# Attention over all contexts: where three transposes of a unit stand, where a row sum stands, and 62 nops in VectorE's program

## The chip, the cores and the metric

The kernel runs on one core of a Trainium2 chip, in one launch. The metric is the device time of that core in microseconds (us). The core has TensorE (matmuls and transposes), VectorE, ScalarE, GpSimd and SyncE (which starts most DMAs). Each engine runs its own program in order, and they wait for each other by semaphores. Every engine's program comes into the engine by DMA while it runs.

## The reference, cut to what matters

The kernel computes a chain of eight residual blocks over x of 16 x 256 x 256 (4096 tokens of width 256), with a context of 16 x 120 tokens of width 192. The change is in the fifth block, an attention in which every token looks at all 1920 context tokens of the batch, in eight heads of width 128:

```python
qh = _split_heads(jnp.einsum('bnq,qi->bni', x, Wq))
kh = _split_heads(jnp.einsum('bmc,ci->bmi', context, Wk))
vh = _split_heads(jnp.einsum('bmc,ci->bmi', context, Wv))
sim = jnp.einsum('hid,hjd->hij', qh, kh) * SCALE
mean = jnp.mean(sim, axis=-1, keepdims=True)
sim = (sim - mean) * ATTN_MATRIX_SCALE + mean
attn = jax.nn.softmax(sim, axis=-1)
out = jnp.einsum('hij,hjd->hid', attn, vh)
return jnp.einsum('bni,iq->bnq', out, Wout) + bout
```

Here `x` is the layer-normed input, and the result is added to it. The blocks before it are an attention with an int8 feed-forward, a second attention and a block of experts; behind it come a ternary feed-forward, a selective block (cross attention that keeps the best 32 scores of a row, with a convolution in frequency space) and an attention over chosen tokens.

## The kernel before

`STAGES` lists the stages; each writes one program for each engine. VectorE's programs of all stages lie one behind the other, so what is added in an early stage moves the code of all later ones. Loops over batches or heads are `Fori` loops of the hardware, whose body is written once and which end in a branch back; the rest is written out. Such loops are at L481 (first stage, 13 passes), L919 (second attention, 14), L1330 and its like (experts, 16), L1642 (heads 1 to 6 of the global attention) and L2371 (selective stage, 5 passes, two batches each).

The changed stage is `global_attention_stage` (L1439). A unit is 512 queries (four token tiles of 128, `QT` = 4) against one head, `n = h * QUADS + t`, with eight units (`QUADS`) to a head and eight heads, so 64 units. The 1920 keys are four chunks of 480 (`chunks`) for the scores and 15 tiles of 128 (`KT`) for the attention. Two units are in work at once, interleaved by token tile j = 0 to 3:

- of unit n+1, `scores(n + 1, ., j)`: four PSUM banks (0 to 3), one for each chunk, three f32r matmuls each (L1849 to L1851). VectorE takes the maximum of each bank (`maximum`, L1695), then of the four, and scales it to the bias of the exponential (L1697, L1698). ScalarE waits for the bias and runs four exponentials (`exponential`, L1801), each with a read of its accumulator that yields the row sum. An exponential frees its bank for the scores of tile j+1, by the semaphore `exped`.
- of unit n, for the key tiles k of this j (`shares[j]`, four of them, three for j = 3): TensorE transposes the probabilities of tile k+2 (`turn`, four 128x128 transposes into bank 4 or 5, L1891) and multiplies tile k with the values, three matmuls into bank 6. ScalarE copies each transposed bank to its f32r high part (`high_probs`, L1780), VectorE takes the low part by a subtraction (`low_probs`, L1689); tile k's matmuls, and the transposes of k+2 into the same bank, wait for its low part (`low_ready`).

At j = 0 TensorE runs all four score banks of unit n+1, then waits until the last exponential of unit n is there (`exped`) and transposes tiles 0 and 1 of unit n; then comes `output(n - 1, 0)`, and then tile 0, which waits for its low part. VectorE at j = 0 does the maximum over all four banks, then `sums` (adds the parts of the row sums and takes the reciprocal, L1719 and L1720), then low 0, low 1, `output(n - 1, 0)` (two operations that add to x_res, L1728), low 2 and so on. At j = 3 TensorE runs the four score banks, transposes tile 14, and multiplies tiles 12, 13 and 14. VectorE at j = 3 does the maximum, then low 14. ScalarE at j = 3 does high 14, then the four exponentials, then the copy of the attention result (L1832).

At j = 2 the queries of unit n+2 are made (`queries`, `high_queries`, `low_queries`). In a head's last unit (`turns_head`, t = 7) the keys of the next head stand where the scores of tile 0 would, and the scores of tile 0 come behind key tile 1; the values of the next head are made in it too. `before` and `after` are false for the first and the last unit of all.

The lines of VectorE's order at L1742 to L1757, and of TensorE's at L1911 to L1922, are those that the change touches:

Of the kernel before, what the change touches and what calls it, by code (L numbers as in the profile page):

```python
# [385 lines left out]
def attention_and_int8_stage(nc, w, ctx):  # L386
# [80 lines left out]

    scores = w.psum[:, 0:per, 0:parts * NCTX].rearrange("p r (k j) -> p r k j", j=NCTX)
    v_bank, k_bank, prob_t_banks, attn_bank, out_bank = 2, 3, (4, 5), 4, 5
    xn_t_bank, q_bank = 6, 7  # L470
    int8_bank = (v_bank, k_bank)
    AHEAD, BEHIND = 5, 6
# [14 lines left out]
    with nc.allow_non_contiguous_dma(reason="rows of a weight for each part"), nc.Block() as block:  # L487
# [57 lines left out]
        @block.vector  # L545
        def _(dve):
            chain = Chain(dve, w.chains["dve"])

            def prepare_weight8():
                dve.wait_ge(weight8_loaded.sem, 16)  # L550
# [888 lines left out]
def global_attention_stage(nc, w, ctx):  # L1439
# [8 lines left out]
    chunks = B // 4  # L1448
    KEYS = B * NCTX
    KT = KEYS // P  # L1450
    QT = 4
# [194 lines left out]
    with nc.Block() as block:  # L1646
# [36 lines left out]
        def _(dve):  # L1683
# [4 lines left out]
                dve.wait_ge(high_is_ready.sem, high_is_ready.count(n))  # L1688
                dve.tensor_tensor(dst, psum, high.bitcast(F32), ALU.subtract).then_inc(ready.sem, 1)  # L1689

            def maximum(n, j):

                for c in range(chunks):
                    dve.wait_ge(scores_psum.sem, scores_psum.count((n * QT + j) * chunks + c))
                    ins = dve.tensor_reduce(top[:, c:c + 1], w.psum[:, c, 0:chunk], AX.X, ALU.max)  # L1695
                chain.link(ins)
                chain.link(dve.tensor_reduce(bias[:, j % 2:j % 2 + 1], top[:, :], AX.X, ALU.max))  # L1697
                dve.tensor_scalar(bias[:, j % 2:j % 2 + 1], bias[:, j % 2:j % 2 + 1], -scale, None,  # L1698
                                  ALU.mult).then_inc(bias_ready.sem, 1)
# [32 lines left out]
            def head(h, first, last):  # L1732
                chain.restart_always()
                for t in range(QUADS):
                    n = h * QUADS + t
                    before, after = not (first and t == 0), not (last and t == LAST)
                    turns_head = t == LAST and after
                    for j in range(QT):
                        if turns_head and j == 0:
                            for c in range(chunks):  # L1740
                                low_keys(h + 1, c)
                        elif after:  # L1742
                            maximum(n + 1, j)
                        if j == 0:
                            sums(n, t)
                        if j == 1 and before:
                            output(n - 1, (t - 1) % QUADS, 1)
                        if j == 2 and not (last and t >= LAST - 1):
                            low_queries(n + 2, t % 2)
                        for k in turned_in[j]:  # L1750
                            if k == 2 and before:
                                if first and t == 1:
                                    dve.wait_ge(bias_added.sem, bias_added.count(0))
                                output(n - 1, (t - 1) % QUADS, 0)
                            if turns_head and k == 4:
                                maximum(n + 1, 0)
                            low_probs(n, k)  # L1757
                            if t == 0 and k == 7:
                                low_values(h, 3, 7)
                            if turns_head and k in (7, 11, 14):  # L1760
                                low_values(h + 1, (7, 11, 14).index(k), 7)
# [82 lines left out]
        def _(pe):  # L1844
# [28 lines left out]
                                     start=(k == 0), stop=(k == DK - 1))  # L1873
                last.then_inc(q_psum.sem, 1)

            def scores(n, par, j, new_keys=None, fresh=False):
                tokens = slice(j * P, (j + 1) * P)
                if j == 0:
                    pe.wait_ge(q_ready.sem, q_ready.count(n))
                for c in range(chunks):  # L1880
                    if new_keys is not None and j == 0:
                        pe.wait_ge(k_ready.sem, k_ready.count(new_keys * chunks + c))
                    else:
                        pe.wait_ge(exped.sem, exped.count((n * QT + j - 1) * chunks + c))
# [21 lines left out]
            def head(h, first, last):  # L1906
                for t in range(QUADS):
                    n = h * QUADS + t
                    before, after = not (first and t == 0), not (last and t == LAST)
                    turns_head = t == LAST and after  # L1910
                    for j in range(QT):  # L1911
                        if turns_head and j == 0:
                            for c in range(chunks):
                                keys(h + 1, c, (n * QT + QT - 1) * chunks)
                        elif after:
                            scores(n + 1, (t + 1) % 2, j)
                        if j == 0:
                            pe.wait_ge(exped.sem, exped.count((n * QT + QT) * chunks - 1))
                            if first and t == 0:
                                pe.wait_ge(v_ready.sem, v_ready.count(2))  # L1920
                            turn(n, t % 2, 0)
                            turn(n, t % 2, 1)  # L1922
                        if j < 2 and before:
                            if j == 0 and t == 0:
                                pe.wait_ge(v_ready.sem, v_ready.count(h * QT + 2))
# [11 lines left out]
                        for k in shares[j]:  # L1937
                            if t == 0 and k % 4 == 0:
                                pe.wait_ge(v_ready.sem, v_ready.count(h * QT + k // 4))
                            pe.wait_ge(low_ready.sem, low_ready.count(n * KT + k))  # L1940
                            if k + 2 < KT:
                                turn(n, t % 2, k + 2)
                            last_mm = three_passes(w.psum[:, 6, :], (v_high[:, k, :], v_low[:, k, :]),
                                                   (prob_t_high[:, k % RING, :], prob_t_low[:, k % RING, :]),
# [1468 lines left out]
```

## Time and profile before

| | us |
|---|---|
| median of 3 runs | 4376.85 (4372.74 to 4380.01) |
| the profiled execution | 4377.85 |
| its span | 4376.0 |
| TensorE busy | 4032.5 (92%) |
| VectorE busy | 3192.7 (73%) |
| ScalarE busy | 2292.7 (52%) |
| GpSimd busy | 557.0 (13%) |

The span is the time from the first to the last instruction of the profiled execution. Busy time is what an engine spends in its instructions; TensorE's matmuls overlap, and the end of one is modelled. The global attention lies between some 1514 and 3364 us of the span, the selective stage's loop between 3629 and 4004 us. In rows of the trace an L-number is a line of the kernel before; "PE" is TensorE, "DVE" VectorE, "ACT" ScalarE; a trailing q is the engine's sequencer, which runs branches and register operations.

### The profile page before, as it was taken

To read this page: it belongs to the slowest core of one execution; us is meant where nothing else is said; L and a number is where in the kernel's file an instruction comes from. 1 tells how busy PE (TensorE), PEld (TensorE's weight loads), DVE (VectorE), ACT (ScalarE), POOL (GpSimd) and SP (SyncE) were. 2 spreads that over 40 slices of the span, in tenths; PEclk is the share of its full clock that TensorE was granted. 3 is DMA by queue.
4 is the path that set the end of the run, shared out by engine and by line. 5 is a ranking of instruction groups with operands and counts; after the bars stand their busy time and mean duration, and the time that the engine had idled before them with its cause. 6 is when DMAs were issued, how large, how long until landed. Compare 5 with 4: busy or idle time off the path is not lost. (4 is left out here: it accounts for less than half of the span.)

```text
span 4376.0 us, 69715 instructions
## 1 busy us (share of the span) xinstructions
PE 4032.5 (92%) x23076; PEld 3186.9 (73%) x23076; DVE 3192.7 (73%) x7663; ACT 2292.7 (52%) x5416; POOL 557.0 (13%) x1081
## 2 busy tenths in 40 slices
PE   6997997999889999999999999999999678889788
PEld 5886775777668777777777777787787456666565
DVE  6996666676657777777777777777777588889457
ACT  3554664555555565555655656555565134444344
POOL 1331001101130000000000000000033422232211
PEclk9998998999989999999999999999999589999899
DMA  3001000000000000000000000000000200000001
GB/s 98 0 0 39 0 0 1 0 0 0 18 4 1 3 3 2 5 1 6 1 2 5 2 5 1 2 5 2 2 1 12 66 1 1 1 1 1 15 27 39
DMA packets 34282, 40.67 MB, mean 9 GB/s; under 512 B 6272, under 2 KB 30474, under 8 KB 33934
## 3 DMA queue, kind: packets, MB, share of 16 engines
q1 hardware_dynamic: 33200, 36.90, 2.9%
q8 instruction: 137, 2.24, 0.2%
q14 instruction: 145, 1.19, 0.1%
q10 hardware_dynamic: 800, 0.33, 0.0%
HBM read 32.77 MB, written 4.19 MB: 8 GB/s over the span
## 5 line engine op out<-in xcount | busy, mean ns | idle before, releaser
L1780 ACT ACTIVATE global_prob_t_high<-psum 128x512 fp32r<-128x512 f32 x960 | 569.8, 601 | 586.9 <-PE psum L1891 586.9
L1689 DVE TENSOR_TENSOR global_prob_t_low<-psum,global_prob_t_high 128x512 fp32r<-128x512 f32 x960 | 656.6, 689 | 252.4 <-ACT global_prob_t_high L1780 238.1
L1695 DVE TENSOR_REDUCE global_top<-psum 128x1 f32<-128x480 f32 x1024 | 666.2, 657 | 115.4 <-PE psum L1851 109.9
L1849 PE MATMUL psum<-global_prob_t_high,global_v_low 128*128 128x512 f32 x960 | 455.7, 475 | 0.8
L1849 PE MATMUL psum<-global_k_high,global_q_low 128*128 128x480 f32 x1024 | 391.2, 382 | 15.0 <-ACT spare L1801 13.0
L1851 PE MATMUL psum<-global_k_high,global_q_high 128*128 128x480 f32 x1024 | 392.1, 383 | 0.0
L1850 PE MATMUL psum<-global_k_low,global_q_high 128*128 128x480 f32 x1024 | 389.1, 380 | 0.0
L1850 PE MATMUL psum<-global_prob_t_low,global_v_high 128*128 128x512 f32 x960 | 379.6, 395 | 0.0
L1851 PE MATMUL psum<-global_prob_t_high,global_v_high 128*128 128x512 f32 x960 | 379.4, 395 | 0.0
L1801 ACT ACTIVATE spare<-psum,global_bias 128x480 f32<-128x480 f32 x512 | 337.1, 663 | 17.5 <-DVE global_bias L1698 16.0
L1801 ACT ACTIVATE global_prob<-psum,global_bias 128x480 f32<-128x480 f32 x512 | 337.2, 662 | 1.3
L1367 ACT ACTIVATE moe_gated<-psum,moe_weight 128x256 f32<-128x256 f32 x512 | 214.8, 471 | 228.6 <-PE psum L1421 213.3
L1891 PEld LDWEIGHTS psum<-ident,global_prob 128*128 128x128 f32 x1920 | 233.6, 141 | 99.3 <-DVE global_prob_t_low L1689 34.6
L1891 PEld LDWEIGHTS psum<-ident,spare 128*128 128x128 f32 x1920 | 233.6, 141 | 96.4 <-DVE global_prob_t_low L1689 33.5
L1891 PE MATMUL psum<-ident,global_prob 128*128 128x128 f32 x1920 | 284.1, 273 | 18.8 <-DVE global_prob_t_low L1689 17.8
L1891 PE MATMUL psum<-ident,spare 128*128 128x128 f32 x1920 | 283.9, 273 | 18.0 <-DVE global_prob_t_low L1689 18.0
L374 POOL COPY powers<-ones 128x128 f32<-128x128 f32 x1 | 0.4, 414 | 1942.6 <-PE psum L1872 1942.6
L1849 PEld LDWEIGHTS psum<-global_k_high,global_q_low 128*128 128x128 f32 x1024 | 194.0, 189 | 56.1 <-ACT spare L1801 14.2
L1850 PEld LDWEIGHTS psum<-global_k_low,global_q_high 128*128 128x128 f32 x1024 | 193.4, 189 | 34.2 <-issue 0.2
L1851 PEld LDWEIGHTS psum<-global_k_high,global_q_high 128*128 128x128 f32 x1024 | 193.7, 189 | 29.5
L1851 PEld LDWEIGHTS psum<-global_prob_t_high,global_v_high 128*128 128x128 f32 x960 | 180.6, 188 | 42.3
L1419 PE MATMUL psum<-moe_we_high,moe_xn_low 128*128 128x512 f32 x512 | 204.3, 399 | 0.0
(486 smaller groups left out, 8335.1 us busy)
## 6 DMA issues: line engine op xcount, KB each, us to landing
x_res<-in_x SPq DMA_DIRECT2D x8, 512.0 KB, 10.1
moe_we<-in_expert_t SPq DMA_DIRECT2D x8, 512.0 KB, 7.5
out<-x_res SPq DMA_DIRECT2D x16, 256.0 KB, 2.1
cho_wqkv<-in_L_ffn_Wqkv SPq DMA_DIRECT2D x2, 1536.0 KB
self_ctx_t<-in_ctx_t SPq DMA_DIRECT2D x2, 1440.0 KB, 13.4
sel_w<-in_L_xattn_W SPq DMA_DIRECT2D x2, 1024.0 KB, 10.4
global_ctx_t<-in_ctx_t SPq DMA_DIRECT2D x1, 1440.0 KB
sel_ctx_t<-in_ctx_t SPq DMA_DIRECT2D x1, 1440.0 KB
```

The costliest lines, as they stand in the source:

```text
L374: pool.tensor_copy(re[:, :, 0], w.ones[:, :])
L1367: last = act.activation(gated[:, local % RING, h, :], w.lane(s)[:, 1 + p % 3, h * D:(h + 1) * D], ACT.Relu, scale=weight[:, s, x:x + 1])
L1419: pe.matmul(bank, xn_low[:, s, k, :], we_high[pair], start=False, stop=False)
L1689: dve.tensor_tensor(dst, psum, high.bitcast(F32), ALU.subtract).then_inc(ready.sem, 1)
L1695: ins = dve.tensor_reduce(top[:, c:c + 1], w.psum[:, c, 0:chunk], AX.X, ALU.max)
L1780: act.activation(dst, psum, ACT.Copy).then_inc(ready.sem, 1)
L1801: act.activation(prob[par][:, j, c * chunk:(c + 1) * chunk], w.psum[:, c, 0:chunk], ACT.Exp, bias=bias[:, j % 2:j % 2 + 1], scale=scale, a ...
L1849: pe.matmul(to, lhs_low, rhs_high, start=start, stop=False)
L1850: pe.matmul(to, lhs_high, rhs_low, start=False, stop=False)
L1851: return pe.matmul(to, lhs_high, rhs_high, start=False, stop=stop)
L1891: last = pe.transpose(w.psum[:, 4 + k % 2, j * P:(j + 1) * P], prob[par][:, j, k * P:(k + 1) * P], w.ident[:, :])
```

## The change

In TensorE's program the transposes of tiles 0 and 1 go from behind the four score banks of token tile 0 to between the third and the fourth, with their wait for the last exponential; the transposes of tile 14 go from behind the four score banks of token tile 3 to between the third and the fourth, with a wait for the low part of tile 12. In VectorE's program low 0 and low 14 go between the maximum of the third and of the fourth bank. Where no scores stand at that place (the head's last unit at j = 0, the last unit of all) the order stays. `sums` goes from j = 0 to j = 2, behind the maximum. ScalarE's program stays. In the first stage, which is `attention_and_int8_stage`, 62 `engine_nop` are put ahead of all else in VectorE's program.

```diff
+    FETCH_FILL = 62
...
             chain = Chain(dve, w.chains["dve"])
+            for _ in range(FETCH_FILL):
+                dve.engine_nop()
...
-            def maximum(n, j):
+            def maximum(n, j, within=None):
 
                 for c in range(chunks):
+                    if within is not None and c == chunks - 1:
+                        low_probs(n - 1, within)
                     dve.wait_ge(scores_psum.sem, scores_psum.count((n * QT + j) * chunks + c))
...
                         elif after:
-                            maximum(n + 1, j)
-                        if j == 0:
-                            sums(n, t)
+                            maximum(n + 1, j, within={0: 0, QT - 1: KT - 1}.get(j))
                         if j == 1 and before:
                             output(n - 1, (t - 1) % QUADS, 1)
+                        if j == 2:
+                            sums(n, t)
...
-                            low_probs(n, k)
+                            if not (after and (k == KT - 1 or (k == 0 and not turns_head))):
+                                low_probs(n, k)
...
-            def scores(n, par, j, new_keys=None, fresh=False):
+            def scores(n, par, j, new_keys=None, within=None):
...
                 for c in range(chunks):
+                    if within is not None and c == chunks - 1:
+                        within()
...
+                    def first_turns():
+                        pe.wait_ge(exped.sem, exped.count((n * QT + QT) * chunks - 1))
+                        if first and t == 0:
+                            pe.wait_ge(v_ready.sem, v_ready.count(2))
+                        turn(n, t % 2, 0)
+                        turn(n, t % 2, 1)
+
+                    def last_turn():
+                        pe.wait_ge(low_ready.sem, low_ready.count(n * KT + KT - 3))
+                        turn(n, t % 2, KT - 1)
...
+                            first_turns()
                         elif after:
-                            scores(n + 1, (t + 1) % 2, j)
-                        if j == 0:
-                            pe.wait_ge(exped.sem, exped.count((n * QT + QT) * chunks - 1))
-                            if first and t == 0:
-                                pe.wait_ge(v_ready.sem, v_ready.count(2))
-                            turn(n, t % 2, 0)
-                            turn(n, t % 2, 1)
+                            scores(n + 1, (t + 1) % 2, j, within={0: first_turns, QT - 1: last_turn}.get(j))
+                        elif j == 0:
+                            first_turns()
...
-                            if k + 2 < KT:
+                            if k + 2 < KT and not (after and k + 2 == KT - 1):
                                 turn(n, t % 2, k + 2)
```

## Rows read from the trace of the kernel before

**Rows 1.** TensorE's timeline, 2149 to 2163 us: start, duration, engine, line, operation.

```profile
2149.13 0.38 PE L1849 MATMUL psum<-global_k_high,global_q_low 128*128 128x480 f32 x1
...
2151.73 0.60 PE L1891 MATMUL psum<-ident,spare 128*128 128x128 f32 x4
...
2153.33 0.40 PE L1851 MATMUL psum<-global_prob_t_high,global_v_high 128*128 128x512 f32 x1
2153.74 0.50 PE L1849 MATMUL psum<-global_prob_t_high,global_v_low 128*128 128x512 f32 x1
...
2154.56 0.37 PE L1849 MATMUL psum<-global_k_high,global_q_low 128*128 128x480 f32 x1
...
2159.62 0.66 PE L1891 MATMUL psum<-ident,global_prob 128*128 128x128 f32 x4 [0.57 <-DVE global_prob_t_low L1689]
2160.04 0.48 PE L1849 MATMUL psum<-global_prob_t_high,global_v_low 128*128 128x512 f32 x1
...
2162.31 0.48 PE L1849 MATMUL psum<-global_prob_t_high,global_v_low 128*128 128x512 f32 x1
```

**Rows 2.** VectorE's timeline from 2145 us; in brackets idle time and who ended it.

```profile
2145.41 0.69 DVE L1689 TENSOR_TENSOR global_q_low<-psum,global_q_high 128x512 fp32r<-128x512 f32 x1 [1.31 <-ACT global_q_high L1780]
...
2149.98 2.61 DVE L1695 TENSOR_REDUCE global_top<-psum 128x1 f32<-128x480 f32 x4
...
2152.82 0.15 DVE L1698 TENSOR_SCALAR global_bias<-global_bias 128x1 f32<-128x1 f32 x1
...
2158.36 0.17 DVE L1719 TENSOR_REDUCE global_inverse<-global_part_sum 128x4 f32<-128x16 f32 x1
...
2158.88 1.29 DVE L1689 TENSOR_TENSOR global_prob_t_low<-psum,global_prob_t_high 128x512 fp32r<-128x512 f32 x2
2160.08 0.86 DVE L1728 SCALAR_TENSOR_TENSOR x_res<-psum,global_inverse,x_res 128x256 f32<-128x256 f32 x2
2160.95 0.69 DVE L1689 TENSOR_TENSOR global_prob_t_low<-psum,global_prob_t_high 128x512 fp32r<-128x512 f32 x1
```

**Rows 3.** ScalarE's timeline over the same seam.

```profile
2152.37 0.60 ACT L1780 ACTIVATE global_prob_t_high<-psum 128x512 fp32r<-128x512 f32 x1 [2.48 <-PE psum L1891]
2153.00 0.66 ACT L1801 ACTIVATE global_prob<-psum,global_bias 128x480 f32<-128x480 f32 x1
2153.56 0.19 ACT L1801 ACTIVATION_READ_ACCUMULATOR global_prob<-psum,global_bias 128x1 f32 x1
...
2154.93 0.67 ACT L1801 ACTIVATE global_prob<-psum,global_bias 128x480 f32<-128x480 f32 x1
...
2160.32 0.60 ACT L1780 ACTIVATE global_prob_t_high<-psum 128x512 fp32r<-128x512 f32 x1 [0.80 <-PE psum L1891]
```

**Rows 4.** A head's first matmul; and TensorE's branches of L1642 (min/median/max ns).

```profile
2057.07 0.48 PE L1849 MATMUL psum<-global_k_high,global_q_low 128*128 128x480 f32 x1 [1.36 <-ACT spare L1801]
...
L1642 PEldq COMPARE_BRANCH  x3: 3446/3557/3897, 1782.2 to 2324.4; - x3
```

**Rows 5.** A pass of the selective loop: busy us of PE, PEld, DVE, ACT, POOL.

```profile
3778.00:3853.00 75.00, 66.69 (x295) 50.20 (x294) 65.63 (x272) 34.30 (x70) 21.95 (x42) 0.98 0.00 1
```

**Rows 6.** Selective loop: VectorE's branches and moves (ns, first and last start), timelines.

```profile
L2371 DVEq COMPARE_BRANCH  x5: 55/63/74, 3701.0 to 4004.0; - x5
L2371 DVEq MOVE  x4: 36/36/36, 3704.0 to 3931.5; - x4
...
3780.85 0.69 DVE L2536 TENSOR_TENSOR spare<-psum,spare 128x512 f32<-128x512 f32 x1 [3.37 <-remote]
...
3781.74 5.38 PE L2769 MATMUL psum<-powers,sel_forward 128*128 128x256 f32 x16 [3.72 <-DVEq L2537]
```

**Rows 7.** Instruction DMAs of that pass; all DMAs, 100 to 315 us.

```profile
q14 instruction: 5, 0.04, 0.2%
...
DMA packets 0, 0.00 MB, mean 0 GB/s; under 512 B 0, under 2 KB 0, under 8 KB 0
```

**Rows 8.** VectorE's timeline early in the kernel.

```profile
20.21 0.29 DVE L265 TENSOR_TENSOR ssm_states<-ssm_states 128x128 f32<-128x128 f32 x1 [12.18 <-DMA ssm_states<-in_c_im_t]
```

## The prediction

> **What bounds the kernel now.** I read first the page's busy times, by which TensorE comes first and VectorE next. Then the three engines' timelines over one seam between two units of the global attention, 2149 to 2163 us [rows 1 to 3]. A unit is 512 queries against one head. Ordinary units (of which the trace holds 48) repeat every 32.00 us, at the full clock of 2.4 GHz. Within one, TensorE runs matmul after matmul but for two places: it waits 0.57 us before the attention of key tile 0 (2159.62, for `low_probs` of tile 0), and it starts tile 14 at 2153.74 where 2153.33 plus a step of 0.23 would allow 2153.56, so 0.18 late. So TensorE bounds most of a unit, and a chain VectorE, ScalarE, VectorE bounds the seam. Last, the selective stage, because the added nops shift VectorE's whole program: there VectorE is busy 65.6 of 75 us [rows 5], the densest engine with its links, and TensorE waits 3.72 us for it in each pass [rows 6].
>
> I count times from P, the first score matmul of token tile 3 (2149.13), in us.
>
> **Part 1, the last transpose earlier.** Now: scores to P+2.60, transposes of tile 14, then attention of 12, 13, 14 [rows 1]; VectorE takes the maximum of the four banks in one go (P+0.85 to P+3.46), the bias is written by the operation at P+3.69, and low 14 runs behind that [rows 2]. After: the transposes go in at the start of the fourth bank, P+1.95 (nine score matmuls of 0.217). ScalarE's high 14 starts 0.64 behind them (2152.37 against 2151.73) and takes 0.60 [rows 3]: P+2.59 to 3.19; low 14 0.03 later for 0.69: P+3.22 to 3.91. VectorE had the third bank done at P+2.81 and idles 0.41. TensorE no longer waits at tile 14, and gains its 0.18. But what is queued behind low 14 is the maximum of the fourth bank, P+3.92 to 4.57 (2.61/4 each); the bias operation starts 0.23 behind it, P+4.80 (it did at P+3.69), so **the bias is 1.11 us later**. Who waits for it: ScalarE's four exponentials, which free the score banks. The first starts 0.18 behind the bias operation (2153.00 against 2152.82), at P+4.98; the others follow in 0.643 steps (2153.00 to 2154.93 is three). Its signal is given when the accumulator read behind it ends, 0.75 after its start, and TensorE starts 0.05 later (as 2159.57 to 2159.62): **P+5.78**. TensorE now starts the next unit at P+5.43, with its bank free since P+4.67; it could after start at P+5.25, but must wait to P+5.78. So the slack of 0.76 is used up and 0.35 is lost here.
>
> **Part 2, the first transposes earlier.** They need the fourth exponential, P+4.98+1.93+0.80 = P+7.71; the banks are paced by the exponentials till then. High 0 starts 0.70 behind, P+8.41 (as 2160.32 behind 2159.62, also from a standing start), low 0 at P+9.04 to 9.73 (now at 2158.88, P+9.75: 0.7 earlier, so TensorE's 0.57 us wait at tile 0 goes). What is late next: the fourth maximum now lies behind low 0, P+9.74 to 10.39; bias operation P+10.62; low 1 0.17 behind it, about as the exponential, P+10.79; `output` 0.61 after low 1 starts (2158.88 and 0.60 per tile to 2160.08), P+11.40; low 2 0.87 later (2160.08 to 2160.95), P+12.27 to 12.96. Now low 2 ends at P+12.51 (2160.95+0.69). TensorE needs it for tile 2, whose attention starts at 2162.31, P+13.18, its transposes 0.35 before. After: transposes at 12.96+0.05 = P+13.01 from a standing start, attention 0.41 later (as 2159.62 to 2160.04 in the same unit): P+13.43. So the attention of tile 2 comes **0.24 us later per unit** than now; behind it TensorE is the bound as before. For 48 units (t = 1 to 6 of eight heads): +11.5 us. Bounds: 0.1 to 0.4 per unit, 5 to 19 us, since eleven hand-overs of a few hundredths each are in the chain.
>
> **Part 3, sums later.** Two small operations and their link, 0.49 us between the bias and low 0 (2158.36 to 2158.88 less the 0.03 hand-over [rows 2]), go behind the third tile's maximum, where VectorE waits 1.31 us for ScalarE's high queries (2145.41): cost nothing; without that cover 0.5 per unit. The gain is already in part 2's chain (without it low 1 would be 0.49 later). In the seven units t = 7, where keys and not scores stand first, it takes some 0.4 off TensorE's wait and meets the 0.35 to 0.45 lost at the unit's start: 0.
>
> **Head boundaries.** At the six back branches of the loop over heads TensorE stands for 1.36 us [rows 4], though the exponential that the row names was long done: TensorE's sequencer is 3.4 to 3.9 us in the branch itself. TensorE reaches the branch when low 14 is there, which comes up to 0.65 earlier; VectorE restarts when it does now. Between 0.2 and 0.47 gain for each, say -2.2 with the seventh; the last unit pays 0.7 for its later exponentials. The attention together: 11.5 + 0 - 2.2 + 0.7 = **+10.0**.
>
> **Part 4, 62 nops.** They stand ahead of VectorE's first work; a little later it idles 12.18 us in a row for a DMA [rows 8], which covers 62 nops of up to 0.19 us each: nothing. What they do is to move all later VectorE code by 62 places. VectorE's instructions come by DMA in blocks of 8 KB, one for every 128 records of its trace. Its loop in the selective stage has 328 records per pass (272 busy ones [rows 5]) and by the fetch times lies over four blocks: 48 records in the first, 36 in the last. At each of its four back branches the branch takes 63 ns, but the next instruction comes 2.98, 2.93, 2.96 and 2.81 us later (3701.0 to 3704.0 [rows 6]), and 5 blocks are fetched in each pass [rows 7]. VectorE's next work waits 3.37 us, and TensorE 3.72 us for VectorE [rows 6], so this is on the path. Moved by 62 (any shift from 48 to 92 would do) the loop lies in three blocks. Do three stay resident, with the fourth fetched ahead? Loops that cross one block edge stay: between 100 and 315 us, twelve passes of a loop whose ScalarE part crosses an edge, nothing is fetched at all [rows 7], so at least three blocks are held. A fourth no row shows; the refetch of all four blocks in every pass fits three or four held. I take the gain, since the loop would then ask for one block less than the smallest number excluded: (11.68 - 4 x 0.14) = **-11.1 us**; bounds 0 and -12.
>
> By the Trainium skill, "Runtime: NRT & Kernel Launch", section "Instruction fetch mechanics", an engine holds 32 KiB in two lines of 256 instructions, and a taken branch outside them stalls for a fetch. The trace differs in the line (8 KB). Read as 32 KiB in 8 KB blocks it is four, and the stall goes; read as only two pages it stays, which is the first rival.
>
> **Sum.** 4377.85 (the profiled execution, span 4376.0; the runs' median is 4376.85) + 10.0 - 11.1 = 4376.8, by the median about **4376**. Within 0.2% (8.8 us) of now, which is about what a measurement can tell from no change.
>
> **Rivals.**
> First, slower: the selective loop's stall stays, as three blocks and the one fetched ahead don't fit. For it: no row shows a loop over three blocks. It decides from the first back branch: if that costs 2.9 us, 4376.85 + 10 = 4387.
> Second, faster: the late bias hides. For it: TensorE's bank is free 0.76 us early now, and the two waits that the change aims at go, 0.57 + 0.18 = 0.75 in some 55 units, 41 us; with the nops' 11 it would be 4325. Against it: bias 1.11 later is more than 0.76. With hand-overs shorter than I take, anything up to 4365.
> Third: the chain costs 0.4 to 0.5 a unit, since TensorE restarts at four banks: 4388 to 4395.
> Fourth: the shift splits loops that lay in one block (attention and experts stages, 27 back branches) and these stall, 27 x 2.9 = 78 us: 4455. Against it the ScalarE loop above.
>
> **Chances.** Forecast 0.45 (4368 to 4386), first rival 0.22, second with all between 0.22, third 0.08, fourth 0.03. Of the forecast a tenth or more lies below 4368. Faster 0.30, same 0.44, slower 0.26. The range leaves out the far ends of the second and the fourth: 4355 to 4391.
>
> **What would show it.** Right: ordinary units 32.24 apart; at the seam TensorE waiting for ScalarE's exponential before the first bank and for low 1 and low 2; no wait at tile 14; the bias of tile 3 at P+4.8; in the selective loop VectorE's move within 0.2 us of the branch. Wrong: units under 32.0 (part 1 hides), or moves 3 us behind the branch (part 4 fails).

## The result, and the profile after

Five runs of each kernel in turn: before 4376.85 us (4372.74 to 4380.01), changed 4357.05 us (4353.84 to 4358.71), ratio 0.9953 with a 95% interval of 0.9939 to 0.9968. The change makes the kernel 0.47% faster. The forecast was 4376, no difference that can be measured; 4357 lies near the lower end of its range, 4355 to 4391, and the case that it took for the likeliest (4368 to 4386) did not come about.

| us | before | changed | difference | forecast |
|---|---|---|---|---|
| the profiled execution | 4377.85 | 4357.05 | -20.8 | -1.1 |
| its span | 4376.0 | 4355.2 | -20.8 | |
| first stage, until TensorE's program of it ends | 355.7 | 359.2 | +3.5 | 0 |
| global attention | 2169.4 | 2168.1 | -1.3 | +10.0 |
| ternary stage | 98.4 | 97.3 | -1.1 | 0 |
| selective stage | 653.6 | 632.3 | -21.3 | -11.1 |
| TensorE, VectorE, ScalarE busy | 4032.5, 3192.7, 2292.7 | 4034.9, 3172.7, 2291.0 | | |

The stages are cut where the drain starts that closes TensorE's program of each. The kernels of the experiments whose attention is that of before took 2169.4 to 2172.0 us for it, so the -1.3 of this row says little; the units below say more. The ternary stage varies as much (96.5 to 99.8 us over all kernels). So almost all of the gain is the selective stage's, where nothing was changed but the place of VectorE's code, and the attention, where all the reordering was done, is as long as before.

**The selective loop.** VectorE's branches and moves of the loop's line (L2390 now), which answer to [rows 6]: minimum, median and maximum in ns, then the first and the last start.

```profile
L2390 DVEq COMPARE_BRANCH  x5: 50/56/74, 3700.5 to 3983.6; - x5
L2390 DVEq MOVE  x4: 36/36/36, 3700.8 to 3913.2; - x4
```

The first branch starts at 3700.5 and the move behind it at 3700.8; before, the pair was 3701.0 and 3704.0. From first to fifth branch it is 283.1 us, before 303.0: a pass takes 70.8 us in place of 75.7 (76.6 the first, 75.5 the others). Busy time in a stretch of 75 us, a pass and a part of the next (columns: PE, PEld, DVE, ACT, POOL, then TensorE's granted clock, DMA share, GB/s), which answers to [rows 5]:

```profile
3773.00:3848.00 75.00, 69.31 (x316) 52.45 (x315) 69.22 (x283) 35.69 (x73) 26.35 (x53) 1.00 0.00 0
```

and all DMA of the same stretch, which answers to [rows 7]:

```profile
DMA packets 0, 0.00 MB, mean 0 GB/s; under 512 B 0, under 2 KB 0, under 8 KB 0
```

No instruction is fetched any more (5 a pass before), and the granted clock is 1.00 where it was 0.98. TensorE at the place where it waited 3.72 us for VectorE:

```profile
3772.77 3.69 PE L2788 MATMUL psum<-powers,sel_forward 128*128 128x256 f32 x16 [1.03 <-DVEq L2556]
```

Its wait is 2.69 shorter, as the gap behind the branch is. But the 16 matmuls behind it take 3.69 us and took 5.38: another 1.69, which the forecast knew nothing of. Before, the granted clock was the lower of the two levels, 1.2 GHz, for a good part of those matmuls:

```profile
3778.00:3781.70 3.70, 0.03 (x1) 0.00 (x0) 0.81 (x2) 0.38 (x1) 0.00 (x0) 1.00 0.01 4
3781.70:3783.70 2.00, 1.96 (x6) 1.66 (x7) 1.67 (x7) 0.00 (x0) 0.87 (x3) 0.66 0.00 0
3783.70:3785.70 2.00, 2.00 (x6) 1.53 (x6) 0.97 (x4) 1.09 (x2) 1.72 (x7) 0.50 0.00 0
3785.70:3787.70 2.00, 1.86 (x11) 1.41 (x9) 1.07 (x2) 0.10 (x1) 1.08 (x3) 0.98 0.00 0
```

These are stretches of the kernel before: 3.70 us with next to no matmul, then 0.66, then 0.50 (1.2 GHz), then 0.98, nearly the full clock again. Together they hold 3.4 us at 1.2 GHz, in which 1.7 us of work are lost, as much as the matmuls took more. Wait and matmuls are 4.4 of the 4.7 us that a pass gained; where the other 0.3 lies was not traced.

**The seam of two units.** TensorE of the changed kernel, P = 2152.14; it answers to [rows 1]:

```profile
2152.14 0.38 PE L1857 MATMUL psum<-global_k_high,global_q_low 128*128 128x480 f32 x1
...
2154.09 0.60 PE L1901 MATMUL psum<-ident,spare 128*128 128x128 f32 x4
...
2157.83 0.49 PE L1857 MATMUL psum<-global_k_high,global_q_low 128*128 128x480 f32 x1 [0.38 <-ACT global_prob L1809]
...
2159.90 1.04 PE L1901 MATMUL psum<-ident,global_prob 128*128 128x128 f32 x8
...
2162.29 0.60 PE L1901 MATMUL psum<-ident,global_prob 128*128 128x128 f32 x4
...
2164.87 0.66 PE L1901 MATMUL psum<-ident,global_prob 128*128 128x128 f32 x4
2165.28 0.48 PE L1857 MATMUL psum<-global_prob_t_high,global_v_low 128*128 128x512 f32 x1
```

and VectorE over the same stretch, which answers to [rows 2]:

```profile
2155.35 0.69 DVE L1694 TENSOR_TENSOR global_prob_t_low<-psum,global_prob_t_high 128x512 fp32r<-128x512 f32 x1 [0.41 <-ACT global_prob_t_high L1788]
2155.96 0.65 DVE L1702 TENSOR_REDUCE global_top<-psum 128x1 f32<-128x480 f32 x1
2156.64 0.16 DVE L1704 TENSOR_REDUCE global_bias<-global_top 128x1 f32<-128x4 f32 x1
2156.83 0.15 DVE L1705 TENSOR_SCALAR global_bias<-global_bias 128x1 f32<-128x1 f32 x1
...
2162.65 0.15 DVE L1705 TENSOR_SCALAR global_bias<-global_bias 128x1 f32<-128x1 f32 x1
2162.75 0.69 DVE L1694 TENSOR_TENSOR global_prob_t_low<-psum,global_prob_t_high 128x512 fp32r<-128x512 f32 x1
2163.35 0.87 DVE L1735 SCALAR_TENSOR_TENSOR x_res<-psum,global_inverse,x_res 128x256 f32<-128x256 f32 x2
2164.14 0.68 DVE L1694 TENSOR_TENSOR global_prob_t_low<-psum,global_prob_t_high 128x512 fp32r<-128x512 f32 x1
```

This is the picture that the forecast drew, step for step: no wait at tile 14, a bias of token tile 3 that is late (P+4.69, before P+3.69), the next unit's scores waiting for ScalarE's exponential (P+5.69), and the attention of tile 2 waiting for low 2. Only it comes at P+13.14 and not at P+13.43, and it was P+13.18 before: the units are 31.96 apart, 0.04 less than before.

### The profile page after: what moved, and what is told of

Its sections match the earlier page's. It is cut to its first block and busy times, and to the rows that moved or that the text cites. A ratio compares the mean times of both kernels' runs of the same rounds, so it can differ in the third digit from the quotient of the medians.

```text
span 4355.2 us, 69783 instructions
## 1 busy us (share of the span) xinstructions
PE 4034.9 (93%) x23076; PEld 3171.0 (73%) x23076; DVE 3172.7 (73%) x7663; ACT 2291.0 (53%) x5416; POOL 563.7 (13%) x1081
## 3 DMA queue, kind: packets, MB, share of 16 engines
q14 instruction: 126, 1.03, 0.1%
## 5 line engine op out<-in xcount | busy, mean ns | idle before, releaser
L1857 PE MATMUL psum<-global_prob_t_high,global_v_low 128*128 128x512 f32 x960 | 445.0, 464 | 0.0
L1857 PE MATMUL psum<-global_k_high,global_q_low 128*128 128x480 f32 x1024 | 406.2, 397 | 32.8 <-ACT spare L1809 21.0
```

The lines of the kernel that those rows point to most:

```text
L1857: pe.matmul(to, lhs_low, rhs_high, start=start, stop=False)
```

## The experiments

Times are medians. The kernels with the 62 nops alone, with the new order alone and with both gains ran four to eleven times, all others once; with these the trace shows where the time went. The kernel before was run again beside each group: 4378.53, 4378.09 and 4380.36 us. "Units" are the ordinary ones (t = 1 to 6) of the looped heads.

**The nops alone.** The kernel before with

```diff
             chain = Chain(dve, w.chains["dve"])
+            for _ in range(62):
+                dve.engine_nop()
```

> The kernel before with the 62 nops and nothing else. Theory (VectorE's code layout makes the selective stage's gain, stall and what follows it): the four passes of the selective loop take 70.8 us as in the changed kernel (75.5 before), VectorE's move comes within 0.3 us of its branch, the stage loses 21.3 us; the first stage is 3.5 us longer, as in the changed kernel, because its VectorE loop now crosses a block edge; the attention's ordinary units stay at 32.00. Sum: 4376.85 - 21.3 - 1.1 + 3.5 = 4358, some 0.43% less than before, and within 3 us of the changed kernel. Rival (the extra 10 us of the selective stage come from somewhere else, such as the attention's new order or an execution's own variation): a gain of about 11 us, 4366. Second rival, on the first stage: its 3.5 us are noise of that execution, then 4354.

Measured: 4360.05 us, ratio to before 0.9956 (0.9943 to 0.997). Passes 70.8, gap 0.25, selective stage 633.5 us. The whole gain of the changed kernel within its uncertainty comes from 62 instructions that do nothing. The first stage ended at 360.4.

**The new order alone.** The changed kernel with

```diff
-    FETCH_FILL = 62
+    FETCH_FILL = 0
```

> The changed kernel with 0 nops: the attention's new order alone. Theory (a unit is 0.03 to 0.05 shorter, not the 0.24 longer that was forecast): units 31.96, the attention stage about 1.3 us shorter than before; selective passes back at 75.5 with a 2.9 us gap behind each branch; time 4376.85 - 1.3 = 4375.5, no difference that can be measured. Rival 1 (the forecast's price of the chain holds, and the execution seen was lucky): units 32.24, 4387. Rival 2 (the order is worth several us, hidden by something that the nops do): 4370 or less.

Measured: 4377.69 us, ratio 0.9998 (0.9988 to 1.0007), units 31.96, attention 2166.9 us, passes 75.5 with gaps of 2.8. The three moves together are worth nothing. Why nothing, when each of them moves something, is what the next three kernels ask.

**The sums alone.** The kernel before with

```diff
-                        if j == 0:
-                            sums(n, t)
                         if j == 1 and before:
                             output(n - 1, (t - 1) % QUADS, 1)
+                        if j == 2:
+                            sums(n, t)
```

> The kernel before with the row sums at token tile 2 and nothing else of the change. Theory (the two operations of the sums stand in the chain that TensorE waits for at key tile 0): low 0 starts 0.49 earlier, TensorE's wait of 0.57 before the attention of tile 0 shrinks to 0.08, and nothing is lost elsewhere, since the maximum and the bias keep their times: ordinary units 31.51, the attention stage 48 x 0.49 = 23 us shorter than before, time about 4354 without any nops. Rival (another chain is right behind, such as output and low 2 on VectorE): units 31.7 to 32.0, and the gain is under half of that.

Measured: 4352.53 us, units 31.57 in looped and written-out heads alike, attention 2142.6 us, 26.8 less than before. TensorE at the seam, P = 2108.87:

```profile
2117.78 1.03 PE L1902 MATMUL psum<-global_wo,global_attn_t 128*128 128x256 f32 x4
2118.92 0.66 PE L1891 MATMUL psum<-ident,spare 128*128 128x128 f32 x4
```

and VectorE:

```profile
2117.99 0.15 DVE L1698 TENSOR_SCALAR global_bias<-global_bias 128x1 f32<-128x1 f32 x1
2118.18 1.29 DVE L1689 TENSOR_TENSOR global_prob_t_low<-psum,global_prob_t_high 128x512 fp32r<-128x512 f32 x2
```

Low 0 starts 0.19 behind the bias operation; before it was 0.64, from this bias operation to the low 0 at 2158.88 [rows 2]:

```profile
2158.24 0.15 DVE L1698 TENSOR_SCALAR global_bias<-global_bias 128x1 f32<-128x1 f32 x1
```

TensorE starts the transposes of tile 2 at P+10.05, before at P+10.49 [rows 1]. All of it reaches the unit: 0.43.

**Sums and first transposes; sums and last transpose.** Both are the changed kernel without nops; the first puts the last transpose and low 14 back, the second the first transposes and low 0. The cores of the two edits, TensorE's alone (VectorE's low 14, or low 0, goes back with them):

```diff
-        scores(n + 1, (t + 1) % 2, j, within={0: first_turns, QT - 1: last_turn}.get(j))
+        scores(n + 1, (t + 1) % 2, j, within={0: first_turns}.get(j))
...
-        scores(n + 1, (t + 1) % 2, j, within={0: first_turns, QT - 1: last_turn}.get(j))
+        scores(n + 1, (t + 1) % 2, j, within={QT - 1: last_turn}.get(j))
+        if j == 0:
+            first_turns()
```

> The changed kernel without the nops and with the last transpose back behind the four banks: sums and the first two transposes alone. Theory (the late bias comes from low 14 ahead of the fourth maximum, so it is gone here, and what the first transposes still cost is low 2, which comes at most 0.2 after TensorE wants it): units 31.5 to 31.6, far below the 31.96 of all three moves. Rival (the first transposes are what costs): units 31.9 or more.

> The changed kernel without the nops and with the first transposes back behind the four banks: sums and the last transpose alone. Theory (the bias 1.0 later paces the next unit's banks by the exponentials, to a fourth bank 0.7 or more later than before; the sums' 0.49 make up for most of it): units 31.8 to 32.0, the late bias of token tile 3 at 4.7 us behind the tile's first score matmul. Rival (the late bias hides in the 0.76 us by which the bank is free early): units 31.4 or less, as TensorE's 0.18 wait at tile 14 goes too.

Measured: with the first transposes 4351.44 us, units 31.58, attention 2143.4; with the last transpose 4377.44 us, units 31.92, attention 2167.3. VectorE at the seam of the second, P = 2152.12:

```profile
2155.34 0.69 DVE L1694 TENSOR_TENSOR global_prob_t_low<-psum,global_prob_t_high 128x512 fp32r<-128x512 f32 x1 [0.41 <-ACT global_prob_t_high L1788]
...
2156.82 0.15 DVE L1705 TENSOR_SCALAR global_bias<-global_bias 128x1 f32<-128x1 f32 x1
```

and TensorE's first matmul of the next unit:

```profile
2157.82 0.48 PE L1857 MATMUL psum<-global_k_high,global_q_low 128*128 128x480 f32 x1 [0.39 <-ACT global_prob L1809]
```

The bias comes at P+4.70 as in the changed kernel, and TensorE waits for the exponential. In the first of the two kernels the wait at tile 0 is gone: the transposes of tile 2 start 0.86 behind the first output matmul, with the sums alone 1.14. But those of tiles 3 and 4 start 0.31 and 0.42 behind the attention matmul ahead of them, with the sums alone 0.23 and 0.24, so 0.26 of the 0.28 is lost again to low 1 and low 2, which come later: the first transposes are worth nothing. So the price of the change is almost all in one of its parts: sums -0.43 a unit, first transposes +0.01, last transpose +0.35 (31.92 against 31.57) or +0.38 (31.96 against 31.58).

| kernel | unit | attention stage |
|---|---|---|
| before | 32.00 | 2169.4 |
| sums | 31.57 | 2142.6 |
| sums, first transposes | 31.58 | 2143.4 |
| sums, last transpose | 31.92 | 2167.3 |
| sums, both (changed, no nops) | 31.96 | 2166.9 |

**How the place of the loop decides: 128, 100 and 40 nops.** Each is the kernel before with another number in `range(...)`.

> The kernel before with 128 nops: the selective loop lies over four blocks of 8 KB again, but with the other parity. Theory (blocks of 8 KB count, and four of them in a loop are too many): passes stay at 75.5, gap 2.9 us, about five instruction fetches a pass. Rival (16 KB lines of 256 instructions, two of which are held, as the Trainium skill, Runtime: NRT & Kernel Launch, section Instruction fetch mechanics, has it): before, the loop lay over three such lines (one block, two, one); moved by half a line it lies over two, and the stall goes: passes 70.8, gap under 0.3 us. First stage: no crossing, so as before (355.7).

> The kernel before with 100 nops. Theory (the loop lies in three blocks for a shift of 48 to 92 only; at 100 its last 8 records reach into a fourth): the stall is back, passes 75.5, gap 2.9 us, although there are more nops than in the changed kernel. Rival (any shift, or the nops as such, help): passes 70.8. Rival of 16 KB lines: by parity either; told together with the kernel of 128 nops. The first stage's VectorE loop crosses no edge at 100 and should end at 355.7 to 356 as before, not at 359.2.

> The kernel before with 40 nops. The forecast's condition was a shift of 48 to 92; 100 works too, so its upper end was wrong by at least 8 places. This asks for the lower end. Forecast's geometry (48 records of the loop in its first block): 8 of them remain in a block of their own, four blocks, passes 75.5, gap 2.9. Corrected geometry (block edges counted back from the fetches of the kernels with 62 and 100 nops, where the edge ahead of the loop stands 35 records before it at 62 nops, so 13 at 40): three blocks, passes 70.8, gap 0.25.

VectorE's branches and moves of the loop with 40 nops:

```profile
L2373 DVEq COMPARE_BRANCH  x5: 55/63/74, 3701.9 to 4003.6; - x5
L2373 DVEq MOVE  x4: 36/36/36, 3704.8 to 3931.4; - x4
```

with 100:

```profile
L2373 DVEq COMPARE_BRANCH  x5: 50/56/74, 3701.9 to 3985.0; - x5
L2373 DVEq MOVE  x4: 36/36/36, 3702.2 to 3914.5; - x4
```

and with 128:

```profile
L2373 DVEq COMPARE_BRANCH  x5: 55/63/74, 3702.7 to 4005.1; - x5
L2373 DVEq MOVE  x4: 36/36/36, 3705.5 to 3932.6; - x4
```

The page's row of fetched blocks in the whole program (packets, MB), with 40 nops (with 128 it is the same row, and 145 before):

```profile
q14 instruction: 146, 1.20, 0.1%
```

and with 100 (the same row with 62):

```profile
q14 instruction: 126, 1.03, 0.1%
```

At 40 and 128 the stall is there (4375.38 and 4379.16 us), at 62 and 100 it is gone (4358.72 us with 100). 128 nops, a whole block, restore the state before, so it is the place within a block of 8 KB that counts, and lines of 16 KB don't: 128 nops move the loop by half such a line, and in one of the two places two such lines would have held it. My expectation for 100 was wrong, and the forecast's own counts show why: with 328 records in the loop and 48 in its first block, 24 and not 36 are left for the fourth (48 + 128 + 128 + 24), so any shift from 48 to 104 would do and not only to 92. The trace with 100 nops agrees: the edge behind the loop shows some 5 records behind its last. The "corrected" count that I then made for 40, from the times of fetches, was wrong as well; these stood up to some 20 records off the edge. With the condition 48 to 104 all four come out: 40 no, 62 yes, 100 yes, 128 no.

**Where the other 2 us of a pass went: a delay without a fetch.** The kernel with 62 nops alone, and in the loop

```diff
             def iteration(M, T, F, now, done):
                 chain.restart_always()
+                if now and not isinstance(now[0], int) and now[1] == 0:
+                    for _ in range(4):
+                        link(dve.tensor_tensor(prod[0], by_cos[:, :, :], by_cos[:, :, :], ALU.mult))
```

> The kernel before with the 62 nops, and at the top of each pass of the selective loop four linked VectorE multiplications of 128x512 that nothing reads (0.69 us each with its link 0.7, so 2.8 us: as long as the stall that the nops took away, 2.98 less 0.25, but without any fetch). It asks where the rest of the 4.7 us per pass went, of which the gap behind the branch is only 2.7. Theory (TensorE's long idle: it waits 3.8 us, its granted clock falls to 1.2 GHz, and the 16 matmuls behind the wait take 5.4 instead of 3.7 us): passes 75.4, PEclk 0.50 in the two us behind the wait. Rival (the rest belongs to the fetches themselves, not to the idle): passes 73.6, the 16 matmuls 3.7 us.

> The same with two multiplications, 1.4 us: TensorE's wait becomes 2.4 us. Theory (the clock falls only behind a longer idle): passes 70.8 + 1.4 = 72.2, clock 1.00 behind the wait. Rival (any idle lengthened costs clock in proportion): passes 73.1. It brackets the idle at which the clock is lost between 2.4 and 3.7 us, or below 2.4.

The added work with four:

```profile
3787.28 2.87 DVE L2536 TENSOR_TENSOR powers<-sel_by_cos 128x512 f32<-128x512 f32 x4 [0.60 <-DVE sel_mean L2527]
```

TensorE's matmuls behind it, with four:

```profile
3791.16 5.27 PE L2774 MATMUL psum<-powers,sel_forward 128*128 128x256 f32 x16 [3.94 <-DVEq L2542]
```

and with two:

```profile
3785.34 6.50 PE L2774 MATMUL psum<-powers,sel_forward 128*128 128x256 f32 x16 [2.49 <-DVEq L2542]
```

Measured: 4386.47 us and passes of 75.1 to 75.4 with four, 4380.61 us and 75.07 with two. The first is as the theory has it: a delay of 2.87 us that fetches nothing costs 4.5 us, and the matmuls take 5.27. So the rest of the loss is the clock's, behind the longer wait, and needs no fetch. The second missed both expectations. With half the delay TensorE's wait is 2.49 us and the pass is just as long, because the 16 matmuls now take 6.50 us. The granted clock of the kernel with two:

```profile
3784.00:3786.00 2.00, 0.66 (x2) 0.60 (x3) 1.80 (x5) 0.00 (x0) 0.00 (x0) 0.55 0.00 0
3786.00:3788.00 2.00, 2.00 (x6) 1.58 (x5) 1.21 (x6) 0.22 (x1) 1.50 (x6) 0.50 0.00 0
3788.00:3790.00 2.00, 2.00 (x6) 1.61 (x5) 0.87 (x2) 0.87 (x2) 1.61 (x7) 0.50 0.00 0
3790.00:3792.00 2.00, 2.00 (x9) 1.60 (x9) 0.54 (x2) 0.00 (x0) 0.56 (x1) 0.74 0.00 0
```

By these rows the clock is at 1.2 GHz for 6.8 us, at least 5.5 of them with TensorE at work, where in the pass of before that is shown above it was 3.4. That is not the shorter wait's doing alone: at the first back branch of the kernel before, behind a wait of 3.78, the matmuls took longer than at the others too,

```profile
3705.21 6.39 PE L2769 MATMUL psum<-powers,sel_forward 128*128 128x256 f32 x16 [3.78 <-DVEq L2537]
```

which is the 1.0 us by which that first pass is the longer. Wait and 16 matmuls together: 1.03 + 3.69 = 4.72 in the changed kernel; 2.49 + 6.50 = 8.99; 3.72 + 5.38 = 9.10 before; 3.94 + 5.27 = 9.21. So 1.46 us more of waiting cost 4.3, and the next 1.45 cost 0.2. At which wait between 1.03 and 2.49 the clock begins to fall was not tried, nor what makes it stay low for 3.4 us in one pass and for longer in another.

**The two gains together.** The kernel before with the sums moved and 100 nops at the start; and with the sums moved and 80 nops ahead of the attention stage's first maximum:

```diff
+            for _ in range(80):
+                dve.engine_nop()
             chain.restart_always()
             for j in range(QT):
                 maximum(0, j)
```

> The kernel before with the sums at token tile 2 and 100 nops. Theory: both gains add, 23 us of the sums and 21 of the selective stage, less 2.4 for the experts' loop that now crosses a block edge: 4377 - 23 - 21 + 2 = 4335, some 1.0% below before and 22 us below the changed kernel. Rival (as for the sums alone, if they gain less than half): 4345 to 4357.

> The kernel before with the sums at token tile 2, and 80 nops not at the start but ahead of VectorE's first maximum in the attention stage, where it idles 6.42 us for TensorE: 80 x 0.028 = 2.3 us are hidden there, and the loops of the first stages and of the experts stay where they were. Theory: attention as with the sums alone (units 31.57), selective passes 70.8, experts' passes 29.34 and not 29.50 as with 100 nops at the start: 4334.4 - 15 x 0.16 = 4332, 1.05% below before. Rival (80 places here don't shift the selective loop as at the start, or the nops delay the stage): 4352 or 4336.

Measured: 4334.43 us (ratio 0.9899, 0.9882 to 0.9915) and 4335.0 us (0.9893, 0.9877 to 0.991). Both beat the kernel before by 1.0% and the changed one by some 22 us. The gains add: attention 2145.3 and 2144.6, selective stage 633.6 and 633.1. With 100 nops at the start the experts' passes take 29.5, with 80 at the later place 29.4, as before (29.3 to 29.4); in 15 passes that is under 2 us, which the times don't resolve: the 4332 expected for the second can't be told from the first. That the loop crosses a block edge is not enough to cost this: with 62 nops its back branch shows the longer gap as well (0.24), and its passes stay at 29.3.

## Where the prediction was right and where wrong, point by point

**The number.** 4357 lies inside the range of 4355 to 4391, but that is luck. Two terms were wrong, and both the same way: the attention was priced 11.3 us too dear, and the gain of the selective stage 10.2 us too small; the first stage's 3.5 us, of which the forecast had none, took a little back. The range reached down to 4355 only for the rival in which the late bias hides, and that rival did not come about.

**What bounds the kernel:** right in kind. The seam of a unit is bound by the chain of VectorE and ScalarE, and the selective stage by VectorE, as read. But the forecast put TensorE's wait at tile 0 at 0.57, the idle time of the row. Where nothing holds TensorE, the transposes start 0.86 behind the first output matmul (2161.43 to 2162.29 in the changed kernel); before, it was 1.59 (2158.03 to 2159.62). The wait was 0.73.

**Part 1, the last transpose:** right. Bias at P+4.80 forecast, P+4.69 measured; next scores at P+5.78 and P+5.69; the slack of 0.76 is overrun, and the wait at tile 14 goes. The kernels with and without this part show its price, +0.35 to +0.38 a unit. The forecast has 0.35 lost at this place, but never gave it as a price of this part by itself.

**Part 2, the first transposes:** the chain is right, its size isn't. It is 0.29 us too long, nearly all in three hand-overs of VectorE to itself: the fourth maximum starts 0.61 behind low 0 and not a full 0.70; low 1 starts 0.10 behind the bias operation and not 0.17; low 2 comes 0.79 behind `output`, not 0.87. Another 0.02 had come in by low 0, the rest in roundings. VectorE starts an operation some 0.08 before the one ahead has ended, where its data are there; the sum had taken this for the step from low 1 to `output` and not for the others. So a unit is 31.96 and not 32.24: 48 x 0.28 = 13.4 us too much.

**Part 3, the sums:** the mechanism is right, and so is the remark that their 0.49 lies in part 2's chain. Measured 0.45 at low 0 and 0.43 a unit. But the forecast priced the three moves as one sum, and so didn't see that this one, done alone, is worth 25 us (4378.09 to 4352.53), and that the last transpose takes most of it back. It was to be had from [rows 2]: ahead of low 0 stand only the sums, and TensorE waits for low 0.

**Head boundaries:** forecast -2.2 and +0.7. Measured: a looped head takes 269.95 us, before 271.24, of which five ordinary units give 0.2; so each boundary gains 1.1. The size is near the forecast's, the reason is another: it had low 14, which comes earlier, let TensorE reach the branch sooner. The three intervals of a head around its boundary are 111.3 us before, 109.7 with the sums alone, 109.7 with sums and first transposes, 110.3 with sums and last transpose, and 110.2 with all three and no nops. So the sums give it, and the last transpose takes back a third or so. The six looped heads together give 7.4 (five passes 6.5, the first head 0.9). Against it the last head, which is written out, loses 3.1: its ordinary units go from 31.83 to 32.01, and its last two, from copy to copy of the attention result, take 1.5 more (49.99 to 51.51). The prologue and the head ahead of the loop lose 3.0, of which the kernel without nops shows 1.4. Together -7.4 + 3.1 + 3.0 = -1.3. The forecast had taken 32.00 for all units. In the last head the sums cost less before, as this stretch of VectorE before shows beside [rows 2]:

```profile
3241.19 0.15 DVE L1698 TENSOR_SCALAR global_bias<-global_bias 128x1 f32<-128x1 f32 x1
3241.26 0.16 DVE L1719 TENSOR_REDUCE global_inverse<-global_part_sum 128x4 f32<-128x16 f32 x1
3241.45 0.18 DVE L1720 RECIPROCAL global_inverse<-global_inverse 128x4 f32<-128x4 f32 x1
3241.66 1.29 DVE L1689 TENSOR_TENSOR global_prob_t_low<-psum,global_prob_t_high 128x512 fp32r<-128x512 f32 x2
```

Bias operation to low 0 is 0.47 here and 0.64 in the loop, with the same operations. In the loop each count that is waited for is worked out from the head's number, by a register operation in front of each wait; that these cost the 0.17 is an inference from the two stretches, and no run here took them away.

**Part 4, the nops:** the main step is right. The stall lay in the four blocks, it goes with three, and the nops themselves cost nothing. The gap gave (11.68 - 0.99) = 10.7 of the forecast's 11.1. The step that failed is the price of the stall: the forecast took its own length, 11.68 less four short branches, and nothing for what stands behind it. Behind it TensorE lost its full clock, and this was to be read in the trace of before, in the 5.38 us that 16 matmuls took right behind the wait [rows 6]. With it a pass gives 4.7, and the first 5.8, and the stage 21.3. The condition's upper end, 92, was a slip in the count (36 records for 24, so 104; 100 works), its lower end, 48, agrees with 40 and 62. Nor did [rows 7] show that at least three blocks are held, as the forecast has it: the loop there crosses one edge and so lies over two. The kernels with 62 and with 100 nops show it.

The traces show blocks of 8 KB, and with 128 nops, half of a 16 KB line, the stall is still there. The rule that the forecast weighed (the Trainium skill, "Runtime: NRT & Kernel Launch", section "Instruction fetch mechanics": 32 KiB as two lines of 256 instructions) has the wrong line for this engine, by these runs. Its 32 KiB, taken as four blocks, agrees with a loop over three that fetches nothing; that four and no more are held no run here shows. The profile's other queue of instruction fetches brings 16 KB a packet, so 8 KB is said of VectorE's alone; whose program comes by it no run here isolates. Of the kernel before (packets, MB):

```profile
q8 instruction: 137, 2.24, 0.2%
q14 instruction: 145, 1.19, 0.1%
```

**The first stage:** forecast 0, measured +3.5. Its loop crosses a block edge with 62 nops, and a pass takes 19.07 in place of 18.96, 1.3 us in 12 passes; ScalarE's loop that crosses an edge, which the forecast cited [rows 7], had shown that nothing is fetched, and I had read this as no cost. The other 2.2 are no larger than what differs from execution to execution: without a nop at the start this stage ended between 355.7 and 359.2 in six kernels, and with 62 between 356.6 and 361.5 in four.

**Rivals.** The second, faster by 4325 to 4365, is where the time came out, but not by its mechanism: the late bias doesn't hide. The first, third and fourth didn't come about. The two mistakes are of like size: the chain that was priced 0.28 a unit too long, and part 4 weighed by the length of the gap alone.

## What to carry to other kernels

Price each part of a change by itself, even those that come together: here one part gave 25 us and another took nearly all of it back. Where an engine's wait is removed, look at how long the same instructions take right behind that wait and elsewhere; if they are slower there, the wait costs more than its length. A loop's place in the instruction stream can cost as much as its work: compare the time from a back branch to the next instruction over the loops of a kernel, and if it is us and not tenths, try shifting the loop with nops in a stretch where its engine idles.

## What the runs showed of the hardware

- VectorE's branch back costs 0.13 us to the next instruction for a loop within one block, 0.23 to 0.25 for one that crosses block edges but is all held, and 2.7 to 3.0 where the first block must be fetched. A loop of 328 records is held for shifts of 62, 80 and 100 places and not for 0, 40 and 128.
- A TensorE wait of 1.03 us left the clock at 2.4 GHz; waits of 2.49, 3.72 and 3.94 us were followed by 1.2 GHz, and the 16 matmuls behind them took 6.50, 5.38 and 5.27 us in place of 3.69. The shortest of the three cost as much as the others. At nearly equal waits the matmuls differ by pass: 6.39 behind 3.78 us, and 5.38 behind 3.72.
- A nop on VectorE takes 0.028 us; the 62 of the changed kernel run from 2.89 to 5.05 us, with one gap of 0.46 among them; no fetch stands there, and what makes it no row shows.
- VectorE's operation of 0.69 on 128x512 lets the next start 0.61 behind its own start where that one's data are there.
